# Batch 1's activation blocks in DRAM: one fp32 copy, split when fetched, instead of two stored parts

## What is computed

```python
x = L0_attn_hidden_states                      # (2, 1024, 512)
h = _layernorm(x, axis=-1)
qkv = jax.nn.silu(h @ qkv_w.T)                 # 32 heads of 128: q, k, v
# per block of tokens, state kv per head:
#   scores = (q k^T) * diag_decay; out = scores v + (q * q_decay) kv
#   kv = kv * block_decay + (k * k_decay)^T v
xf = attn * rsqrt(mean(attn * attn) + EPS)
gate = jax.nn.sigmoid(h @ gate_w.T)
x = x + _layernorm((gate * norm_w * xf) @ out_w.T)
x = x + _layernorm(ffn(_layernorm(x)))         # silu(gate) * up, then down
```

## Time and profile before

| | |
|---|---|
| median of 3 executions | 2412.8 us (2411.97 to 2414.72) |
| the profiled execution | 2410.65 us, of which the span from first to last instruction is 2408.5 |
| busy in the span | PE 98%, weight loads 83%, GpSimd 70%, VectorE 58%, ScalarE 50% |
| granted TensorE clock, mean | 0.997 of full speed |
| chain that ended last | PE 86%, DMA 4%, ACT 3%, DVE 3%, POOL 2% |
| DMA | 307.15 MB, 128 GB/s over the span |
| fetches of the blocks, 7 x 1024 KB | issued from 1019.3 to 1034.6 us, 7.1 to 15.4 us to landing |

### The profile page before, as it was taken

The page is one execution under the profiler, slowest core; times in us unless marked ns, Lnnn a source line. Parts: engine busy times, 40 slices in busy tenths (PEclk is TensorE's granted clock), DMA queues, the critical chain, the costliest instruction groups (busy, mean ns, idle before and its releaser), DMA issues.

```text
span 2408.5 us, 38344 instructions
## 1 busy us (share of the span) xinstructions
PE 2352.5 (98%) x12276; PEld 2003.7 (83%) x12276; DVE 1390.7 (58%) x2475; ACT 1207.0 (50%) x1748; POOL 1678.1 (70%) x1322
## 2 busy tenths in 40 slices
PE   6999999999999999989999999999999999899997
PEld 5788888888888888878888888888888888788886
DVE  5555555565666666656565555555555555565655
ACT  5555555555444444435554555444444444366563
POOL 4677777777777777756777777777777776464675
PEclk9999999999999999999999999999999999999999
DMA  3444443444444444464444343443333334512212
GB/s 127 126 136 137 132 131 125 142 142 142 136 138 131 134 142 136 148 209 146 135 136 129 125 132 127 139 140 127 118 112 107 112 109 142 182 54 79 79 62 96
DMA packets 165953, 307.15 MB, mean 128 GB/s; under 512 B 22384, under 2 KB 102256, under 8 KB 163184
## 3 DMA queue, kind: packets, MB, share of 16 engines
q1 hardware_dynamic: 138992, 269.93, 34.6%
q10 hardware_dynamic: 26880, 36.18, 4.6%
HBM read 219.02 MB, written 87.03 MB: 127 GB/s over the span
## 4 chain that ended last, share of the span: by engine, by line
PE 86%; DMA 4%; ACT 3%; DVE 3%; issue 2%; POOL 2%; SPq 0%; DVEq 0%; ACTq 0%; POOLq 0%
PE proj L1995 53%; PE yp L1995 17%; PE sc L2042 4%; PE sc L2065 4%; PE sc L2068 4%; PE sc L2055 3%; DMA k_blocks<-pd 1%; DMA v_tok<-v_blocks 1%; ACT piece L1006 0%; DMA nw<-norm_w 0%; DVE pd L1498 0%; ACT L915 0%; ACT k L915 0%; DMA fs_stage<-ffn_scales 0%; ACT w_even L877 0%
## 5 line engine op out<-in xcount | busy, mean ns | idle before, releaser
L1995 PE MATMUL proj<-xb,w_odd 128*128 128x512 f32 x2694 | 703.4, 399 | 7.1 <-DVE g L1461 3.0
L1995 PE MATMUL proj<-xb,w_even 128*128 128x512 f32 x2694 | 679.4, 396 | 17.2 <-DVE xb L1413 5.0
L1995 PEld LDWEIGHTS proj<-xb,w_even 128*128 128x128 f32 x2694 | 497.5, 189 | 119.5 <-issue 9.7
L1995 PEld LDWEIGHTS proj<-xb,w_odd 128*128 128x128 f32 x2694 | 488.5, 188 | 105.5 <-DVE q L1469 4.8
L599 POOL TENSOR_TENSOR qd<-q,table 128x512 f32<-128x512 f32 x128 | 164.0, 1294 | 194.2 <-ACT q L915 194.2
L1543 DVE TENSOR_TENSOR g<-sc,g 128x512 f32<-128x512 f32 x128 | 88.4, 691 | 298.1 <-ACT sq L929 298.0
L590 POOL TENSOR_TENSOR ow_lo<-v_tok,ow_hi 128x1024 fp32r<-128x1024 f32 x32 | 76.6, 2394 | 235.7 <-ACT ow_hi L883 235.7
L1550 DVE TENSOR_TENSOR y<-yp,y 128x512 f32<-128x512 f32 x240 | 164.2, 684 | 121.1 <-PE yp L1995 120.2
L1995 PE MATMUL proj<-x_t,f_hi 128*128 128x512 f32 x896 | 214.2, 392 | 2.5 <-issue 2.5
L1995 PE MATMUL yp<-ow_hi,g_hi 128*128 128x512 f32 x512 | 202.5, 396 | 1.3 <-DVE y L1550 1.3
L584 POOL TENSOR_TENSOR w_odd<-ws,w_odd 128x1024 fp32r<-128x1024 f32 x63 | 151.2, 2400 | 72.4 <-ACT w_odd L877 72.4
(11 more groups left out here) (193 smaller groups left out, 4418.6 us busy)
## 6 DMA issues: line engine op xcount, KB each, us to landing
raw<-w_attn SPq DMA_DIRECT2D x128, 512.0 KB, 3.6
k_blocks<-pd SPq DMA_DIRECT2D x64, 512.0 KB, 3.5
k_tok<-k_blocks SPq DMA_DIRECT2D x256, 128.0 KB, 2.8
v_blocks<-vf SPq DMA_DIRECT2D x64, 512.0 KB, 2.7
v_tok<-v_blocks SPq DMA_DIRECT2D x256, 128.0 KB, 2.8
v_tok<-w_out SPq DMA_DIRECT2D x32, 512.0 KB, 4.4
fraw<-w_ints SPq DMA_DIRECT2D x13, 1024.0 KB, 4.9
piece<-w_ints ACTq DMA_DIRECT2D x21, 512.0 KB, 4.3
```

The lines of the kernel that those rows point to most:

```text
L1995: last = pe.matmul(psum, s, m, start=start and n == 0, stop=n == len(terms) - 1, skip_group_check=more)
```

## The change

The stores write the mixed piece once, in fp32 (`x_blocks` loses its axis of two parts, and half its bytes). The high copy and the low subtraction leave the windows 1 to 8. In window 15 the fetch brings 512 KB into the low half of `xb`, ScalarE copies it rounded into the high half (`fetched_hi`), and VectorE subtracts in place (`fetched_lo`). PE's products of K in window 16 wait for VectorE's counter instead of the transfer. The places of the fetches and of V's second read on SyncE's queue change.

```diff
+        xb_hi_done, xb_lo_done = sem("xb_hi_done"), sem("xb_lo_done")
-        x_blocks = nc.dram_tensor("x_blocks", (NB, P, 2, RT, SEG), F32).ap()
+        x_blocks = nc.dram_tensor("x_blocks", (NB, P, RT, SEG), F32).ap()
+        fetch_order = (B_11, T_2, T_3, B_21, T_1, B_22, T_4)
             def activations(b, i):
                 sp.wait_ge(proj_done, products_until(PAIRS - 1, GG, i))
-                sp.wait_ge(piece_hi_out, 16 * 2 * CH)
-                sp.wait_ge(piece_lo_out, 16 * 2 * CH)
-                sp.dma_start(xb[:, b].bitcast(F32), x_blocks[b]).then_inc(xb_in[b], 16)
+                sp.wait_ge(piece_out, 16 * 2 * CH)
+                sp.dma_start(xb[:, b, 1].bitcast(F32), x_blocks[b]).then_inc(xb_in[b], 16)
...
-            def split_piece(j):
-                pool.wait_ge(piece_hi_done, j + 1)
-                pool.tensor_tensor(piece_lo.bitcast(F32R), piece_lo, piece_hi.bitcast(F32),
-                                   ALU.subtract).then_inc(piece_lo_done, 1)
...
-            def piece_high(j):
+            def store_piece(j):
                 act.wait_ge(piece_mixed, 4 * (j + 1))
-                act.activation(piece_hi, piece_lo,
-                               ACT.Copy).then_inc(piece_hi_done, 1)
-            def store_high(j):
-                act.wait_ge(piece_hi_done, j + 1)
-                act.dma_start(piece_blocks[0, j],
-                              piece_hi.bitcast(F32).rearrange("p (b n) -> p b n", b=NB)).then_inc(piece_hi_out, 16)
-            def store_low(j):
-                act.wait_ge(piece_lo_done, j + 1)
-                act.dma_start(piece_blocks[1, j], mix[:, :, :]).then_inc(piece_lo_out, 16)
+                act.dma_start(piece_blocks[j], mix[:, :, :]).then_inc(piece_out, 16)
+            def fetched_hi(b):
+                act.wait_ge(xb_in[b], 16)
+                act.activation(xb[:, b, 0], xb[:, b, 1].bitcast(F32), ACT.Copy).then_inc(xb_hi_done, 1)
...
+            def fetched_lo(b):
+                dve.wait_ge(xb_hi_done, fetch_order.index(b) + 1)
+                lo = xb[:, b, 1]
+                dve.tensor_tensor(lo, lo.bitcast(F32), xb[:, b, 0].bitcast(F32),
+                                  ALU.subtract).then_inc(xb_lo_done, 1)
...
                 if x_wait:
-                    pe.wait_ge(xb_in[b], 16)
+                    pe.wait_ge(xb_lo_done, fetch_order.index(b) + 1)
```

More of the change, by code:

```diff
@@ L448, in window @@
                 if second_batch:
-                    activations(B_11, 1)
+                    activations(T_2, 6)
                 v_read(w, 0)
                 if second_batch:
-                    activations(T_2, 6)
                     activations(T_3, 7)
+                    activations(B_21, 2)
+                    activations(T_1, 5)
+                    v_read(w, 1)
+                    activations(B_22, 3)
+                    activations(T_4, 4)
                 if next_weights:
@@ L743, in _ @@
             first_window()
[L744 to L747, removed]
+            window(1, first=True)
+            with pool.Fori(2, PAIRS - 1) as w:
                 window(w)
@@ L1045, in window @@
             def window(w, next_weights=True, checks=None, first_done=False, finish=None, begin=None,
-                       part=None, next_part=None, into_ffn=False):
+                       part=None, next_part=None, into_ffn=False, fetch=False, fetched=False):
                 a = w - 1
@@ L1056, in window @@
                 activate(w, KK, OUT11)
+                if fetched:
+                    fetched_hi(B_22)
                 keep_s1(w, QQ)
+                if fetched:
+                    fetched_hi(T_4)
                 if part is not None:
@@ L1113, in window @@
                 keep_s1(w, GG)
+                if fetch:
+                    fetched_hi(B_11)
                 activate(w, VV, OUT22)
@@ L1120, in window @@
                 activate(w, VV, OUT21)
-                if part is not None:
-                    store_low(part)
+                if fetch:
+                    fetched_hi(T_2)
                 if into_ffn:
@@ L1130, in window @@
                 activate(w, GG, OUT22)
+                if fetch:
+                    fetched_hi(T_3)
                 if next_part is not None:
@@ L1139, in window @@
                     split_hi_a(w + 1, QQ)
+                if fetch:
+                    fetched_hi(B_21)
                 activate(w, GG, OUT21)
+                if fetch:
+                    fetched_hi(T_1)
             def split_hi_plain(kind):
@@ L1645, in window @@
                 update_state(a, 0, 1)
+                if fetched:
+                    fetched_lo(B_22)
                 if rms_of is not None:
@@ L1651, in window @@
                 keep_s3(w, KK)
+                if fetched:
+                    fetched_lo(T_4)
                 scale_out_weights(a)
@@ L1691, in window @@
                 finish_21(w, VV)
+                if fetch:
+                    fetched_lo(B_11)
                 keep_s2(w, GG)
@@ L1694, in window @@
                 decay_scores(w, 0, 1)
+                if fetch:
+                    fetched_lo(T_2)
                 if checks is not None:
@@ L1706, in window @@
                 decay_scores(w, 1, 1)
+                if fetch:
+                    fetched_lo(T_3)
                 if begin is not None:
@@ L1713, in window @@
                 turn_v(w, 0, 1)
+                if fetch:
+                    fetched_lo(B_21)
                 if ends_first:
@@ L1718, in window @@
                 add_out(a, 7, first)
+                if fetch:
+                    fetched_lo(T_1)
                 if next_part:
```

46 lines of the change are left out of this document (17 added, 29 removed).

## The result

The changed kernel takes 2417.89 us in the median (2413.53 to 2421.4, 11 executions); the kernel before, beside it on the same chip, 2411.97 (2407.37 to 2414.72, 11). The ratio is 1.0023, 95% interval 1.0016 to 1.0031: some 5.5 us slower, between 3.9 and 7.5. That lies inside the range given. The difference of the two medians, 5.9, is 0.25% of the time, just past the bound of 0.2% for "no difference", and the interval has that bound inside.

A forecast was written before the change was run, and what follows sets the result against it. PE, busy 98% of the span, was taken as the bound, with 8.6 us lost to the fetches. Pieces 0 and place of the fetches +3.4 gave 2416.2 us against the median 2412.8; range 2410 to 2422.

The forecast's parts named there:

- Pieces: Windows 1 to 8: removed ScalarE copies, GpSimd subtractions and stores gain 0 us, since PE waits for none of them.
- rival D: The change shows in windows 1 to 8: short idle times go, 4 us in all, 2412.2; chance 0.03.
- Steps 1 and 2: Window 15 fetches: B_11 lands in 3.6 us, ScalarE 2.3 late; T_2 lands in 4.2, its subtraction ends at 1028.1.
- rival A: Slower by over 0.2%: T_2 lands later than 5.6 us, reaching QQ4 one to one; 2419.1 to 2421.5; chance 0.33.
- Step 3: Window 15: VectorE's sum of G ends at 1032.3, behind T_2's subtraction, so PE newly waits 5.0 us before GG3.
- the look: VectorE's look at a block of integers behind T_2's subtraction in window 15, counted as 1.20 + 1.19 us.
- Steps 4 and 5: ScalarE and VectorE alternate to 1046.2; in window 16 new waits eat the 8.6 us, KK4 starts when it did.
- the clock counted 0: Half clock after the 5.0 us wait falls on GG3 to KK6, where PE has time: 0, upper end 1.7 us.
- the walk: The step-by-step chain through windows 15 and 16; overturned if PE's position at KK4 differed from 1054.7 by over 2 us.
- Step 6: Window 16: maximum 5.3 us late, 8.05 of reduction, V sums begin at 1055.8; PE starts QQ4 3.4 us late.
- B: Faster by over 0.2%: fetch lies beside other work, both old waits and slow clock go, 8.6 us, 2404.2; chance 0.10.
- C: No effect at QQ4: GpSimd's 8.05 us gap is not the reduction, V sums start in time; 2412.5; chance 0.05.

The follow-up runs named there:

- e2: Changed kernel with GpSimd's reduction over the partitions moved behind the V sums in window 16; +6.9 us to the kernel before, ratio 1.0018 to 1.0039.
- e5: Changed kernel without GpSimd's reduction (maxima go through DRAM as a row, VectorE takes the maximum); +0.9 us to the kernel before, ratio 0.9998 to 1.0016.
- e4: Kernel before, fetching only the high half of each block (512 KB), batch 0's low parts used; -0.6 us to the kernel before, ratio 0.9987 to 1.0005.
- e7: Kernel before with half of each fetch and without GpSimd's reduction; -5.1 us to the kernel before, ratio 0.9970 to 0.9988.
- e3: Changed kernel with T_2's split behind G's sums and GpSimd's reduction behind the V sums; +5.6 us to the kernel before, ratio 1.0014 to 1.0033.
- e1: Changed kernel with only T_2's copy and subtraction moved back behind G's sums; +4.0 us to the kernel before, ratio 1.0006 to 1.0024.
- e6: Kernel before without GpSimd's reduction (maxima go through DRAM as a row, VectorE takes the maximum); +0.5 us to the kernel before, ratio 0.9995 to 1.0013.
- e8: Changed kernel without GpSimd's reduction, splits spread into idle places, VectorE's window 16 steps reordered; -3.4 us to the kernel before, ratio 0.9975 to 0.9993.
- e9: The spread version without reduction, with T_3's and B_21's copies and T_3's subtraction moved earlier; -3.6 us to the kernel before, ratio 0.9977 to 0.9995.

## Why the prediction was right, and where it was not

The forecast was +3.4 us and the range 2410 to 2422; the measured +5.9 lies 2.5 above the forecast. Its shape was right: next to nothing from the pieces, a new wait before GG3, the fetches' waits gone, and a delay through GpSimd to QQ4. By its steps, counted from GG1:

- **Pieces, 0.** PE's waits for the normalised piece are 2.0 us between 120 and 600, against 1.7 in the same stretch of the kernel before. In this pair of profiles windows 1 to 8, from KK1 of window 1 to KK1 of window 9, take 518.3 us before and 518.0 after. Over all twelve they take 517.8 on average in the four kernels with two stored parts (516.8 to 518.3) and 516.9 in the eight with one (516.2 to 518.0). So a gain of near 0.9 us is likely and not shown, and it is far from the 4 us of rival D.
- **Steps 1 and 2, the landings.** B_11 was issued at 1014.38, where GG1 ends, as the step says, and landed in 4.35 instead of 3.6. T_2 landed in 4.90 instead of 4.2. All seven have a median of 5.1 us to landing. So both terms were mis-sized by 0.7, and T_2's subtraction ended 1.4 late. The estimate of 3.2 by the Trainium skill ("DMA: Bandwidth & Descriptors", the anatomy of one DMA) is off by more. The page gives its fit for a transfer issued by GpSimd. The rows of this kernel, issued by SyncE with other transfers under way, differ from the estimate by 1.2 and 1.7. The measurement decides. Against rival A: T_2's landing stayed under 5.6.
- **Step 3, GG3's wait.** 5.06, forecast 5.0. Partly luck: the second operation of the look took 0.16 us, where the step counted 1.19 from the earlier trace rows. That figure is a mean over twenty-one operations which took from 0.39 to 4.44 us; the one at this very place had taken 1.85 in the kernel before. The 1.0 gained here made up for most of the 1.4 by which T_2's subtraction was late.

```profile
1029.50 1.23 DVE L1630 TENSOR_TENSOR xb<-xb 128x1024 fp32r<-128x1024 f32 x1 [6.65 <-ACT xb L1013]
1030.64 1.21 DVE L1545 TENSOR_REDUCE maxima<-piece 128x1 f32<-128x1024 int32 x1
1031.89 0.16 DVE L1548 TENSOR_TENSOR maxima<-maxima 128x1 f32<-128x1 f32 x1
...
1042.61 2.02 DVE L1630 TENSOR_TENSOR xb<-xb 128x1024 fp32r<-128x1024 f32 x1 [3.22 <-ACT xb L1013]
...
1049.84 0.11 DVE L1792 TENSOR_REDUCE maxima<-maxima 128x1 f32<-128x3 f32 x1
```

- **Steps 4 and 5, the clock counted 0.** This is the term that failed most. The step said that PE at 1.2 GHz falls where PE has time to spare. It fell on GG3 and the output projections behind it and made GG4 2.4 us later, and ScalarE's weight copy waits for GG4: 1.33 us before 1040.77. B_21's copy behind it was 1.7 late and its subtraction took 2.02 for 1.23. The maximum came 2.4 after the step's time (1049.84 less the 1.23 by which GG1 is later is 1048.6, forecast 1046.2). KK4 came 2.1 later than before; the text had put 2 as the point at which the walk would be overturned. It was passed by 0.1, and by the clock, not by another chain: KK4 follows GG4 by 18.9 us in the changed kernel, in e2 and in e5 alike, and it is from GG3's start to GG4's that these differ, 5.2, 4.2 and 4.4 us, where the kernel before takes 2.8.
- **Step 6, GpSimd.** The place and the direction were right, the mechanism was not. The step took the 8.05 us behind the reduction as its length, and let it begin when the maximum is there. In fact GpSimd has two holes, one ahead of the reduction (7.48 in the earlier trace rows, which the step passed over) and one behind it, and the first does not end with the maximum: see e4. Counted from when GpSimd is free, the V sums start 15.9 us later before and 16.6 after. In this pair alone the two readings can't be told apart: GpSimd is free 7.7 us later from GG1 than before, and the maximum is there 7.8 later. It is e4, with GpSimd free when it was and the maximum 4.5 us sooner, whose V sums come 2.6 later instead of sooner, that speaks against the step's reading. On the forecast's own walk GpSimd would be free at 1038.6 + 1.8 = 1040.4, and the sums at 1056.3, so the wrong reading cost only 0.5 there. The other part of the 3.1 us by which the sums were later than forecast is the clock and the landings, which freed GpSimd 1.9 later than the walk has it, and a hole 0.7 longer. QQ4 then came 5.8 late, forecast 3.4.

The rivals: B (2404.2) is out, though e7 shows that 5.1 of its 8.6 us were there to be had. C is out. A named slower by over 0.2%; its mechanism, T_2's landing, gave 0.7 of its 1.4 us, and the time came out at its edge. That +5.9 lies in the range is in part luck: the clock was counted 0, GpSimd's hold was misread, and the look's short second step took 1.0 off.

Left open is what GpSimd does in the two holes. The Trainium skill ("GPSIMD Engine Reference", section 2.1, instruction dispatch) says that the first call of a freshly loaded kernel pays some 6 us for loading code, with no instruction in the profile. The traces agree in kind (5.52 and 5.53 us ahead of the reduction in e2 and e3, where the maximum was there beforehand), and show more than that: there is a hole on both sides, and the one ahead is not of one length. The stretches of it, e2 and the kernel before, e4 and e1, and last the hole behind the reduction in the changed kernel:

```profile
1048.62:1054.14 5.52, 4.10 (x24) 3.30 (x23) 5.20 (x10) 2.10 (x3) 0.00 (x0) 1.00 0.07 22
```
```profile
1034.59:1042.07 7.48, 3.56 (x21) 2.80 (x20) 2.43 (x6) 1.76 (x2) 0.00 (x0) 1.00 1.04 333
```
```profile
1033.91:1045.13 11.22, 10.34 (x54) 8.42 (x53) 5.21 (x13) 2.96 (x4) 0.00 (x1) 1.00 0.82 284
```
```profile
1038.40:1048.52 10.12, 5.68 (x22) 4.85 (x23) 8.61 (x18) 4.88 (x6) 0.00 (x1) 0.83 0.89 303
```
```profile
1053.11:1060.17 7.06, 5.65 (x32) 4.58 (x31) 5.09 (x8) 2.60 (x3) 0.00 (x0) 1.00 0.00 0
```

With the DMA engines at 7% the hole ahead is 5.52 us, at 82% and more 7.5 to 11.2. That could be code which comes by DMA and queues with the fetches, but it was argued and not tried: no run changed the traffic alone, the shortest of the three long ones stands at the highest DMA share, and the first 6.4 us of the hole before and in e1 also pass before the maximum is there. Against it for the hole behind: it is 7.06 us in the changed kernel while the DMA engines move nothing. The cause stays open. That the V sums, or in e2 and e3 the next work, start 12.8 to 18.6 us after GpSimd is free (e2 the least, e1 the most) is read from the traces, and that this is the path of the changed kernel is shown by e5, e6 and e7.

## What to carry to other kernels

When an edit takes a wait away, look on every engine for the next thing that ends just behind it, and ask from when its time runs: here 1.7 us of slack on ScalarE stood between a saving of 6 us and nothing, and only taking away both showed either. When work is put into an engine's fixed order ahead of a transfer's landing, the landing is paid by all that stands behind it; put the step where the data have long been there. When an edit moves several things to win, as e8 does, run each alone before the gain is given to one of them. And a long "issue" gap on both sides of a short GpSimd operation belongs to that operation: count the engine as held from the moment it is free, or let VectorE do the job, which here was worth 5 us in one kernel and nothing in the other.

## What the hardware did unexpectedly

- A maximum of 128 numbers over the partitions, 0.38 us in most profiles' own line, kept GpSimd from all other work for 12.8 and 13.5 us where the numbers were ready beforehand (e2, e3), and for 15.9 to 18.6 where part of that time also passed before they were.
- After an idle time of 5.06 us PE's next 5.22 us ran at a granted clock of 0.51, after 3.92 us the next 8.20 at 0.79: 2.6 and 1.7 us lost beside the wait itself. But the loss does not follow the length of the wait: after 3.18 us (e6, before KK2) the next 8.20 ran at 0.63, 3.0 lost; after 1.99 us (e9) the next 4.41 at 0.61, 1.7 lost; and after 2.63 us (e8) the clock of the next 3.4 stayed at 1.00.
- A 512 KB fetch of a block takes 4.35 and 4.90 us (B_11, T_2) and 5.1 in the median of seven, from 4.3 to 6.8, where 3.6 and 2.9 were read for the same size.
